# Unrolling a causal attention phase, moving its diagonal mask from TensorE to VectorE, and another order of its jobs

## What is computed

```
xn = layernorm(x)
Q, K, V = (xn @ W.T).reshape(b, s, 16, 16).transpose(0, 2, 1, 3)      for each of W_q, W_k, W_v
scores = einsum('bhqd,bhkd->bhqk', Q, K) * 16 ** -0.5
scores = where(tril, scores, -inf)
out = softmax(scores) @ V
s = out.transpose(0, 2, 1, 3).reshape(b, s, 256) @ W_o.T
g = silu(two layers of windowed attention and gated feed-forward of xn)
x + s * g
```

## Time and profile before

| | |
|---|---|
| median of 3 runs | 2124.43 us (2120.41 to 2127.48) |
| profiled execution, its own time | 2127.53 us |
| span of the profile | 2125.7 us |
| granted TensorE clock, mean | 0.942 |
| busy: PE / DVE / ACT / POOL | 89% / 71% / 57% / 45% |
| projection, to the causal phase's first load | 0 to 136.5 us |
| causal phase | 136.5 to about 690 us |
| two layers of window and feed stages | to about 2050 us |
| output | to the end |

### The profile page before, as it was taken

How to read it: one execution, slowest core, us unless ns; L and a number is a source line. 1 busy time by engine, 2 the same in 40 slices (tenths; PEclk the granted TensorE clock), 3 DMA queues, 4 the chain that set the end, 5 groups by cost and what they waited for, 6 DMA issues and landing times. The chain is left out here.

```text
span 2125.7 us, 44153 instructions
## 1 busy us (share of the span) xinstructions
PE 1902.0 (89%) x13472; PEld 1376.4 (65%) x13472; DVE 1504.3 (71%) x3610; ACT 1208.7 (57%) x2501; POOL 961.0 (45%) x789
## 2 busy tenths in 40 slices
PE   5769999999997699999996999779999999699976
PEld 4633433343442588888885788668888887578865
DVE  5657778786882598989995554269898999555424
ACT  3314656565666477777774434257777777443323
POOL 3441112121121677777771433267777777143320
PEclk9868999999999799999997999879999999799988
DMA  5791645645540100000022121200000002212137
GB/s 203 270 213 27 90 66 72 87 68 74 78 62 21 47 28 28 26 25 25 25 68 65 30 59 50 93 13 25 25 25 25 25 26 69 62 30 59 51 117 244
DMA packets 165019, 143.35 MB, mean 67 GB/s; under 512 B 31298, under 2 KB 145406, under 8 KB 164734
## 3 DMA queue, kind: packets, MB, share of 16 engines
q1 hardware_dynamic: 163518, 140.14, 28.0%
q10 hardware_dynamic: 1344, 1.31, 0.2%
HBM read 90.80 MB, written 50.35 MB: 66 GB/s over the span
## 5 line engine op out<-in xcount | busy, mean ns | idle before, releaser
L654 DVE TENSOR_REDUCE ca_mx<-ca_pR 128x1 f32<-128x512 f32 (+3 forms) x768 | 375.8, 549 | 90.8 <-PE ca_pR L524 47.8
L631 ACT ACTIVATE ca_pr<-ca_pS 128x1024 f32<-128x1024 f32 (+3 forms) x384 | 300.4, 813 | 242.8 <-PE ca_pS L548 184.0
L811 POOL TENSOR_TENSOR w_tsn<-w_qk,w_tab 128x512 f32<-128x512 f32 x128 | 260.2, 2052 | 188.6 <-DVE w_pn L1009 171.9
L888 ACT ACTIVATE w_pe<-w_sm,w_nmax 128x256 f32<-128x256 f32 x512 | 253.3, 497 | 151.3 <-DVE w_nmax L1000 151.3
L463 POOL TENSOR_SCALAR_AFFINE_SELECT ca_pr<-ca_pr 128x256 f32<-128x256 f32 x256 | 103.9, 406 | 429.3 <-ACT ca_pr L631 427.0
L521 PE MATMUL ca_pR<-ca_ks,ca_qs 96*128 96x512 bf16 (+3 forms) x768 | 240.7, 350 | 18.9 <-DVEq L707 16.3
L1000 DVE CUSTOM_DVE_ANT_0 w_sm<-w_pS,masks 128x256 f32<-128x256 f32 x512 | 185.9, 420 | 31.9 <-PE w_pS L1184 19.4
L548 PE MATMUL ca_pS<-ca_qs,ca_ks 98*128 98x512 bf16 (+3 forms) x768 | 191.6, 333 | 15.1 <-issue 13.1
L521 PEld LDWEIGHTS ca_pR<-ca_ks,ca_qs 96*128 96x128 bf16 x768 | 73.4, 99 | 186.5 <-DVE ca_mx L654 125.4
L819 POOL TENSOR_TENSOR w_rs<-w_ssc,mhalf 128x16 f32<-128x16 f32 x64 | 187.5, 2930 | 5.3
L1009 DVE TENSOR_SCALAR w_pn<-w_pe,w_rsum 128x256 f32<-128x256 f32 x512 | 182.8, 419 | 4.6
(11 more groups left out here) (163 smaller groups left out, 4416.4 us busy)
## 6 DMA issues: line engine op xcount, KB each, us to landing
QKP<-p_parts SPq DMA_DIRECT2D x32, 384.0 KB, 3.3
ca_qs<-QKP SPq DMA_DIRECT2D x96, 128.0 KB, 6.5
ca_ks<-QKP SPq DMA_DIRECT2D x96, 128.0 KB, 7.0
VA<-p_vaug SPq DMA_DIRECT2D x8, 1024.0 KB, 5.4
ca_va<-VA SPq DMA_DIRECT2D x16, 512.0 KB, 10.6
w_xt<-X SPq DMA_DIRECT2D x64, 128.0 KB, 2.0
X<-w_x SPq DMA_DIRECT2D x64, 128.0 KB, 1.7
f_hh<-X SPq DMA_DIRECT2D x32, 256.0 KB, 4.7
```

What stands on the lines that cost most here:

```text
L631: act.activation(pr[:, k % 2, pair, :, 0:w], pS[:, pair, :, 0:w], ACT.Exp, scale=CS).then_inc(p_ready, 1)
L654: dve.tensor_reduce(mx[:, i, h, ch:ch + 1], pR[jb % RING][:, 0:w], AX.X, ALU.max, negate=True).then_inc(ring_free, 1)
L811: pool.tensor_tensor(dst, src[:, :, ::-1, :], s, ALU.mult).then_inc(S["ts_ready"], 1)
L888: ins = act.activation(pe_[:, h], sm[:, n], ACT.Exp, bias=nmax[:, n:n + 1], scale=-1.0, accum_out=sums[:, h:h + 1])
```

## The change

- `phase_causal` and VectorE's part of the window stage are written out without loops. The loops of the other engines and phases stay.
- The mask on the diagonal of the row maxima is no longer added by a matmul. In the 32 jobs on the diagonal VectorE adds a float32 mask (`later`) while it takes the maximum (`tensor_tensor_reduce`, the operation that the window stage uses), and writes the masked scores to `masked`. In front of it stands a semaphore increment that carries the wait.
- V goes through DRAM without the padding: 512 KB for each group of the projection, 256 KB for each batch of the causal phase, in pieces of 1 KB and 2 KB. It lands in `ca_vin`, and GpSimd copies it into the widened `ca_va` one iteration ahead, before its cuts of step 2. The ones and zeros are written once.
- The order: PER and EARLY give other counts, eight jobs are early instead of seven and they begin in step 9 instead of 10, the late output stands in step 2 instead of 1, and where the jobs of a step stand among scores and value product is a pair for each step (PLACES).

```diff
--- before.py
+++ after.py
@@ -69,14 +69,13 @@
 
-    qs, ks, va, _ = K.stacks
+    qs, ks, vin, _, _ = K.stacks
     parts = QKP[n].rearrange("(z h d) c s -> z c d h s", z=2, h=GH)
...
         out += [(qs[rows, u], parts[0, a]), (ks[rows, u], parts[1, k])]
-    va_t = VA.rearrange("(b t p) (g c) -> b g p t c", b=BATCH, p=P, g=CG)
-    return out + [(va[:, u], va_t[n // CG, n % CG])]
+    return out + [(vin[:, u], VA[n // CG, n % CG])]
 
@@ -161,9 +160,9 @@
                         for transfer in stack_transfers(K, QKP, VA, 0, 0)[g * share:(g + 1) * share]:
-                            sp.dma_start(*transfer).then_inc(K.stacks[3][0], 16)
+                            sp.dma_start(*transfer).then_inc(K.stacks[4][0], 16)
                 sp.wait_ge(v_copied, ONE + 2 + s * 2 + 2)
-                sp.dma_start(va_t[s], vaug[:, j].rearrange("p n h w -> p n (h w)")).then_inc(v_stored[j], 16)
+                sp.dma_start(va_t[it, j], vst[:, j]).then_inc(v_stored[j], 16)
 
@@ -201,8 +200,6 @@
                 rstd_of(0, 0)
-                pool.memset(vaug[:, :, :, :, CD + 1:VW], 0.0).then_inc(v_preset, 1)
-                pool.memset(vaug[:, :, :, :, CD:CD + 1], 1.0).then_inc(v_preset, 1)
 
@@ -296,8 +292,8 @@
                         dve.wait_ge(v_stored[j], ONE + it * 16)
-                    dve.tensor_copy(vaug[:, j, 2 * v:2 * v + 2, :, 0:CD],
-                                    pV[:, v].rearrange("p n (h w) -> p n h w", w=CD)).then_inc(v_copied, 1)
+                    dve.tensor_copy(vst[:, j, :, 2 * v:2 * v + 2],
+                                    pV[:, v].rearrange("p n (g c) -> p g n c", g=CG)).then_inc(v_copied, 1)
 
@@ -347,9 +343,9 @@
     NJ = len(MAXJOBS)
-    PER = [6, 5, 4, 4, 5, 5, 5, 5, 2, 0, 0, 0]
-    EARLY = {10: (0, 3), 11: (3, 7)}
-    A, B = 2, 3
+    PER = [7, 5, 3, 3, 5, 5, 4, 7, 1, 0, 0, 0]
+    EARLY = {9: (0, 2), 10: (2, 5), 11: (5, 8)}
+    PLACES = [(2, 4), (2, 3), (1, 1), (0, 1), (1, 3), (1, 4), (2, 3), (1, 4), (9, 9), (9, 9), (9, 9), (9, 9)]
     NEARLY = max(end for _, end in EARLY.values())
@@ -357,10 +353,10 @@
     OUT_STEP = 5
-    LATE_STEP = 1
+    LATE_STEP = 2
+    SPREAD_AT = 2
     RJ = NJ + 3
     HALF = SEQ // 2
-    LOOPS = (ITERS - 2) // SLOTS
 
@@ -403,8 +399,9 @@
 
-        qs, ks, va, loaded = K.stacks
-        mask_q = sb("ca_mask_q", [P, P], BF16)
+        qs, ks, vin, va, loaded = K.stacks
+        later = sb("ca_later", [P, 512], F32)
+        masked = sb("ca_masked", [P, RING, 512], F32)
         mx = sb("ca_mx", [P, TPB, GH, 2], F32)
@@ -422,7 +419,7 @@
         s_ready, p_ready, pv_done = sem("ca_s_ready"), sem("ca_p_ready"), sem("ca_pv_done")
-        cut = sem("ca_cut")
+        cut, va_preset, va_ready = sem("ca_cut"), sem("ca_va_preset"), sem("ca_va_ready")
         ot_copied, rec_done = sem("ca_ot_copied"), sem("ca_rec_done")
@@ -432,30 +429,40 @@
             first()
-            step(0, 0, 0, False, 2)
-            with e.Fori(0, LOOPS) as it:
-                for u in range(1, SLOTS + 1):
-                    step(it * SLOTS + u, u % SLOTS, it + u // SLOTS, True, 2)
-            for n in range(LOOPS * SLOTS + 1, ITERS):
-                step(n, n % SLOTS, n // SLOTS, True, min(ITERS - 1 - n, 2))
+            for n in range(ITERS):
+                step(n, n % SLOTS, n // SLOTS, n > 0, min(ITERS - 1 - n, 2))
 
...
         def _(pool):
-            pool.memset(mask_q[:, :], 0.0).then_inc(made, 1)
+            pool.memset(later[:, :], 0.0).then_inc(made, 1)
             pool.memset(mx[:, :, :, :], BIG).then_inc(made, 1)
...
 
-            pool.affine_select(out=mask_q[:, :], in_=mask_q[:, :], compare_op=ALU.is_ge, fill=NEG,
+            pool.affine_select(out=later[:, 512 - P:512], in_=later[:, 512 - P:512], compare_op=ALU.is_ge, fill=NEG,
                                base=0, pattern=[[-1, P]], channel_multiplier=1).then_inc(made, 1)
...
                 pool.wait_ge(ones, ONE + u + 1)
+            heads = va[:, :, :, :].rearrange("p u t (h w) -> p (u t h) w", w=VW)
+            pool.memset(heads[:, :, CD + 1:VW], 0.0).then_inc(va_preset, 1)
+            pool.memset(heads[:, :, CD:CD + 1], 1.0).then_inc(va_preset, 1)
+
+            def spread(u, it):
+
+                pool.wait_ge(loaded[u % SLOTS], ONE + (it + 1 + u // SLOTS) * LOADS * 16)
+                pool.sem_inc(K.passed, 1)
+                pool.tensor_copy(va[:, u % SLOTS].rearrange("p t (h w) -> p t h w", w=VW)[:, :, :, 0:CD],
+                                 vin[:, u % SLOTS].rearrange("p t (h d) -> p t h d", d=CD)).then_inc(va_ready, 1)
+
+            spread(0, 0)
             for s, n in K.starts:
...
                 for i, k in enumerate(DIAGONAL):
+                    if i == SPREAD_AT and more:
+                        spread(u + 1, it)
                     for pair in range(2):
@@ -517,12 +524,8 @@
                 bank = ring(*job)
-                diag = k0 + w == (i + 1) * P
-                ins = pe.matmul(bank[:, 0:w], qs[0:SHIFT_ROW, u, h, i * P:(i + 1) * P],
-                                ks[0:SHIFT_ROW, u, h, k0:k0 + w], start=True, stop=not diag)
-                if diag:
-                    ins = pe.matmul(bank[:, w - P:w], K.identb[:, :], mask_q[:, :], start=False, stop=True)
-                ins.then_inc(ring_full, 1)
+                pe.matmul(bank[:, 0:w], qs[0:SHIFT_ROW, u, h, i * P:(i + 1) * P],
+                          ks[0:SHIFT_ROW, u, h, k0:k0 + w], start=True, stop=True).then_inc(ring_full, 1)
 
@@ -556,6 +559,9 @@
                 pe.wait_ge(p_ready, ONE + 2 + n * 2 * NSTEP + 2 * k + 2)
+                if k == 0:
+                    pe.wait_ge(va_preset, ONE + 2)
+                    pe.wait_ge(va_ready, ONE + n + 1)
                 if k in DIAGONAL:
@@ -604,17 +610,17 @@
 
+                    first_ones, next_ones = PLACES[k]
                     scores(n, u, k, 0)
-                    do(at[k][:A])
+                    do(at[k][:first_ones])
                     scores(n, u, k, 1)
-                    do(at[k][A:B])
+                    do(at[k][first_ones:next_ones])
                     if k:
...
                         weighted(n - 1, (u - 1) % SLOTS, NSTEP - 1)
-                    do(at[k][B:])
-
-            pe.wait_ge(made, ONE + 3)
+                    do(at[k][next_ones:])
+
             run(pe, first, step)
@@ -651,8 +657,15 @@
                 dve.wait_ge(ring_full, ONE + n * RJ + jb + 1)
-                dve.tensor_reduce(mx[:, i, h, ch:ch + 1], pR[jb % RING][:, 0:w], AX.X, ALU.max,
-                                  negate=True).then_inc(ring_free, 1)
+                if ch * 512 + w == (i + 1) * P:
+
+                    dve.sem_inc(K.passed, 1)
+                    dve.tensor_tensor_reduce(masked[:, jb % RING, 0:w], pR[jb % RING][:, 0:w], later[:, 512 - w:512],
+                                             -1.0, BIG, ALU.add, ALU.min, mx[:, i, h, ch:ch + 1])\
+                       .then_inc(ring_free, 1)
+                else:
+                    dve.tensor_reduce(mx[:, i, h, ch:ch + 1], pR[jb % RING][:, 0:w], AX.X, ALU.max,
+                                      negate=True).then_inc(ring_free, 1)
 
@@ -1060,11 +1073,8 @@
 
-            with dve.Fori(0, NW // TPB - 1) as seq:
-                for t in range(TPB):
-                    step(seq * TPB + t, t % 4, seq * 2 + t // 4, t)
-            for t in range(TPB):
-                step(NW - TPB + t, t % 4, (NW - TPB + t) // 4, t)
+            for w in range(NW):
+                step(w, w % 4, w // 4, w % TPB)
 
@@ -1755,7 +1765,7 @@
         QKP = nc.dram_tensor("QKP", [BATCH * CG, P, 3, SEQ], BF16, kind="Internal").ap()
-        VA = nc.dram_tensor("VA", [TOK, CH * VW], F32, kind="Internal").ap()
+        VA = nc.dram_tensor("VA", [BATCH, CG, P, TPB, GH * CD], F32, kind="Internal").ap()
         AO = nc.dram_tensor("AO", [TOK, D], F32, kind="Internal").ap()
```

More of the change, by code:

```diff
@@ L105, in phase_project @@
         rest = sb("p1_rest", [P, CG, SUP * P], F32)
-        vaug = sb("p1_vaug", [P, 2, SUP, CH, VW], F32)
+        vst = sb("p1_vst", [P, 2, CG, SUP, GH * CD], F32)
         pT = ps("p1_pT", [P, KD, 512], F32)
@@ L120, in phase_project @@
         part_stored = [sem(f"p1_part_stored{i}") for i in range(CG)]
-        v_ready, v_copied, v_preset = sem("p1_v_ready"), sem("p1_v_copied"), sem("p1_v_preset")
+        v_ready, v_copied = sem("p1_v_ready"), sem("p1_v_copied")
         v_stored = [sem(f"p1_v_stored{i}") for i in range(2)]
         x_t = x.rearrange("(s n p) d -> s p n d", n=SUP, p=P)
-        va_t = VA.rearrange("(s n p) c -> s p n c", n=SUP, p=P)
+        va_t = VA.rearrange("b g p (f n) c -> b f p g n c", f=2)
         block = c.enter_context(nc.Block())
@@ L249, in _ @@
         def _(dve):
-            start_at_one(dve, mine + K.stacks[3])
+            start_at_one(dve, mine + K.stacks[4])
             dve.sem_inc(rest_ready, CG)
@@ L280, in first @@
                 lo_of(0, 0)
-                dve.wait_ge(v_preset, ONE + 2)
             def step(s, j, it, final):
@@ L1809, in program @@
```

(1 more changed line is left out.)

## The result

The changed kernel takes 2137.28 us in the median of 4 runs (2137.04 to 2138.99), against 2124.69 (4 runs) for the kernel before: 1.0063 of it, with a 95% interval of 1.0045 to 1.008. It is slower by 12.6 us, a small difference but outside the spread of the runs; the prediction said 2102 and faster. The profiled execution took 2137.04 us.

What follows compares the result with a forecast made beforehand. TensorE's busy time was taken to hide waits for VectorE's row maxima to free ring banks. Terms -14.6 - 5.2 + 2.6 - 3.4 + 2.0 - 4.2 = -22.8 us gave 2102 us; eight in ten, 2086 to 2117.

Steps and rivals of the forecast that it cites:

- The loops: Straight code saves 14.6 us at the causal phase's loop jumps and 5.2 at VectorE's in the window stage.
- the rival of late fetching: Straight code fetched late undoes or doubles the 14.6 us: 2117 to 2131; chance 0.06, shared with V's copy or the spread.
- The mask on VectorE: Diagonal maxima: TensorE loses 1.9 us an iteration, VectorE gains 0.012 us per 512-column job, 0.03 on average.
- V's copy on GpSimd: Causal phase, one 512-element copy per iteration, placed one iteration ahead: 0 us; 0.4 to 2 a time if cover failed.
- The start of the phase: Causal phase's first maxima, bound by VectorE: one more job, diagonal ones and a wider memset, +2.0 us (0.6 to 3.9).
- The projection: Less V traffic in the DMA queue at the projection's tail: -4.2 us (from -2 to -6).
- The first and the last interval: Causal phase: the first interval saves 0.9 us and the last 2.5, together -3.4.
- The meeting on the DMA queue: Causal phase: loads start later, wanted sooner; TensorE waits in step 9, 31.6 us an iteration, 13 x 0.2 = +2.6.
- leg from store to early job: Causal phase: 15.8 us from store to the loads' end, then 0.3 until TensorE starts; 16.1 in all.
- The leg from early job to store: Causal phase, first early job to output's store: 14.0 to 14.1 us of VectorE work, 15.5 in all.
- With 1.4 over, 15.5: In the stretch from early job to store, 1.4 us beyond VectorE's work; before the change 1.12 over.
- The clock: Rival: TensorE's step 9 gap of 1 to 2.5 us brings half clock in 13 iterations, +32 us, 2134; chance 0.09.

Runs made afterwards that it cites:

- experiment 4: The kernel before with both loops written out and nothing else changed: 2104.56 us, ratio 0.9907.
- experiment 9: The changed kernel with its eight early jobs in steps 10 and 11 instead of 9 to 11: 2102.90 us, ratio 0.99.
- experiment 3: The changed kernel with eleven extra matmuls, results overwritten, ahead of the wait for the loads: 2116.36 us, ratio 0.9964.
- experiment 10: The changed kernel with five extra matmuls of 512 columns ahead of the wait for the loads: 2124.35 us, ratio 0.9999.
- experiment 6: The changed kernel with the order of jobs of the kernel before; straight code, mask on VectorE and unpadded V stay: 2098.38 us, ratio 0.989.
- experiment 5: The changed kernel with the late output, and the loads behind it, in step 3 instead of 2: 2161.73 us, ratio 1.0193.
- experiments 1: The changed kernel with the late output, and the loads behind it, put back into step 1: 2094.14 us, ratio 0.9853.

## Why the prediction was wrong, step by step

**Right in kind and size.** The loops: 19.8 us forecast, 20.1 measured in experiment 4, and the longest "issue" wait of TensorE in the changed kernel from 200 to 640 us is 0.8 us, so the rival of late fetching is out. The mask on VectorE: 0.60 to 0.61 us for 512 columns, as forecast. No engine is seen to wait for V's copy on GpSimd. The start of the phase: first load to first shift copy was 30.1 us and is 31.5, +1.4 for +2.0.

**Right in kind, off in size.** The projection gave 6.1 us, not 4.2. The first and the last interval, 31.20 and 30.25 us, were to save 3.4 together and saved 0.9.

**The meeting on the DMA queue** was seen: the loads start a step later and are wanted a step sooner, the early job is what is late, and the wait stands just where it was said to. Its leg from store to early job was 16.1 us forecast and is 16.37: the last load lands 16.33 us behind the store, not 15.8, and TensorE starts 0.05 us later, not 0.3. The leg from early job to store is where a size failed: "With 1.4 over, 15.5". It is 16.36 at full clock. VectorE's work in it, 14.0 to 14.1, was counted rightly, the copy of the shift with it; the time in which VectorE has nothing to do was taken as 1.4 and is 2.3. It had been read (1.12) from a kernel whose first early job stood in step 10. With the early jobs in steps 10 and 11 the same sum gives 14.9, the shift's 0.60 taken off, and experiment 9 measures 15.02. So the estimate was fair for that order; two early jobs in step 9 brought TensorE's scores and value product of that step into the chain, and with them the wait of 0.84 us. This and the other leg are 0.86 + 0.27 = 1.13 us an iteration, some 15 in all, and by themselves would have made some 2116, an estimate: still faster, as experiment 3 is.

**The clock** is the step that turned the sign. The prediction held against its rival that "the new gap is shorter than the 3.36 us one that left the clock alone". The argument takes one gap that did no harm as a bound for all shorter ones. Also, 3.36 us is the time from one matmul's start to the next; idle, as the waits here are counted, TensorE was 2.98 us. That is the shortest of the three jumps' gaps. The two others came with half clock, the first in the earlier trace rows; they are, TensorE before, and the clock behind the second (windows):

```profile
300.79 1.03 PE L548 MATMUL ca_pS<-ca_qs,ca_ks 98*128 98x512 bf16 x2 [3.50 <-issue]
...
497.60 1.03 PE L548 MATMUL ca_pS<-ca_qs,ca_ks 98*128 98x512 bf16 x2 [3.14 <-issue]
```

```profile
498.00:506.00 8.00, 8.00 (x39) 3.00 (x38) 5.22 (x9) 3.94 (x5) 1.45 (x4) 0.60 0.01 3
```

And in experiment 10 a gap of 1.44 us is already followed by half clock. The rival gave 2.5 us a turn and 2134 in all. The time is near that, but by a smaller price on a longer chain: 1.37 us by experiment 3, or 1.53 by the legs of the changed kernel (17.89 against 16.36), 18 to 20 us in all. Its chance of 0.09 was much too low, since a wait for loads in each turn was itself held likely and of the two gaps looked at one had brought the clock down. That the time came out near this rival's 2134 is in part luck: its price of 2.5 us was too high by about what the chain's 1.13 us makes up.

**The sum.** Against 2104.7 us for the profiled execution it is: 13 iterations at 34.18 for 31.6, +33.5; first and last interval +2.5; start -0.6; projection -1.9; together +33.5, where 2137.04 is +32.3. The last 1.2 us lie behind the last copy of the shift, where 6.3 us were saved for the 5.2 forecast.

**What stays open.** What decides whether a gap brings the clock down is not settled. It is not the gap's length alone: of two gaps of 2.02 us in the changed kernel the one at 292.12 did and the one at 325.97 did not, in experiment 10 one of 1.44 us did, and the kernel before had one of 2.98 us that didn't. Nor was it tried why single loads took longer than others (17.65 us from store to early job once, against 15.9 to 17.2). And no run has V's way alone: what it is worth is known only together with the mask (experiment 6) or from the landing of the loads.

## What to carry to other kernels

When loads are issued behind a piece of work in an engine's order, moving that piece moves the loads, and the first reader may be moving the other way in the same edit; add up the cycle from reader to reader, and count in each leg the work of every engine whose step it now crosses. A wait of TensorE that comes once in a turn can be priced twice, as the gap and as the slow clock after it, and here a gap of 1.44 us was enough; a single gap that did no harm is no bound. The cure that was worth most here is to give the transfer its own condition for starting: the loads put behind a wait of their own on the issuing queue gave 52 us, and the order that had looked bad was then the better one (30.04 us an iteration for 31.13).

## What was unexpected of the hardware

Half clock came with TensorE gaps of 1.44 to 4.03 us: in 12 of 13 turns of the changed kernel, 4 of 13 of experiment 10 and all 13 of experiment 5. After no wait for the loads of 1.37 us or less, in experiments 1, 3, 9 and 10, did it come. After the gap of 2.59 us it came about a microsecond after work had begun again (395.36, and 0.70 in the window of 396); in the gap of 3.80 us it came before. It cost the leg 1.5 us where the clock over the 8 us was 0.79, and 2.6 to 3.1 where it was 0.65 or 0.57. Useless work can pay: eleven matmuls whose results are thrown away made the changed kernel 20.9 us faster.

Straight code of 16 iterations ran with no "issue" wait over 0.8 us from 200 to 640 us, where a loop's jump back had cost 3 to 6 us.
